# A graph network on one core: a sort's one-hot tables compared in f32, and registers of the message loop loaded one tile earlier

## The reference

```python
out = relu(n_feat @ lin0_w.T + lin0_b)
h = out
eh = relu(e_feat @ en1_w.T + en1_b)
w_e = (eh @ en2_w.T + en2_b).reshape(-1, D, D)
for _ in range(STEPS):                       # STEPS = 6
    msg = einsum('ei,eio->eo', out[src], w_e)
    agg = segment_sum(msg, dst, num_segments=n_nodes) + conv_bias
    m = relu(agg)
    h = gru_cell(m, h, gru_wih, gru_whh, gru_bih, gru_bhh)
    out = h
```

## Time and profile before

| | us |
|---|---|
| median of 3 runs | 36292.2 |
| lowest, highest | 36284.42, 36300.33 |
| the profiled execution | 36308.66 |
| its span, first to last instruction | 36306.9 |
| PE busy (matmuls) | 27537.1 |
| DVE busy | 25689.6 |
| ACT busy | 12361.2 |
| POOL busy | 28544.6 |

### The profile page before, as it was taken

The page is one execution under the profiler, slowest core; times in us unless marked ns, Lnnn a source line. Parts: engine busy times, 40 slices in busy tenths (PEclk is TensorE's granted clock), DMA queues, the critical chain, the costliest instruction groups (busy, mean ns, idle before and its releaser), DMA issues. The chain is left out here.

```text
span 36306.9 us, 436242 instructions
## 1 busy us (share of the span) xinstructions
PE 27537.1 (76%) x89048; PEld 15722.1 (43%) x89049; DVE 25689.6 (71%) x33878; ACT 12361.2 (34%) x38546; POOL 28544.6 (79%) x30158
## 2 busy tenths in 40 slices
PE   4443356655663333699999999999999999999999
PEld 2110034455663333444444444444444444454444
DVE  6654422222531211599999999999999999999998
ACT  0000011111200000255555555555555555555554
POOL 5777777677237677699979997999799979988997
PEclk6555566655655555799999999999999999999999
DMA  2221122211310010111111111111111111111111
GB/s 50 49 47 28 28 65 81 64 27 28 92 28 14 13 15 14 33 48 49 49 45 49 48 49 46 48 49 49 45 49 49 47 47 49 48 43 50 49 49 43
DMA packets 1456734, 1613.34 MB, mean 44 GB/s; under 512 B 955316, under 2 KB 1117095, under 8 KB 1348519
## 3 DMA queue, kind: packets, MB, share of 16 engines
q1 hardware_dynamic: 743256, 1078.25, 9.4%
q0 software_dynamic: 645120, 473.02, 7.5%
q10 hardware_dynamic: 68192, 60.43, 0.6%
HBM read 1365.34 MB, written 246.33 MB: 44 GB/s over the span
## 5 line engine op out<-in xcount | busy, mean ns | idle before, releaser
L2123 PE MATMUL l3m_p_w<-en,l3m_hid 128*128 128x512 f32 x39936 | 19533.7, 617 | 177.2 <-DVE l3m_prod L2204 101.8
L2193 DVE TENSOR_REDUCE l3m_xg<-l3m_prod 128x32 f32<-128x1056 f32 x9984 | 12427.1, 1245 | 0.3
L2014 POOL DMA_INDIRECT l3m_xg<-wide_table,l3m_mt x9984 | 9806.3, 982 | 2444.4 <-issue 1547.1
L2204 DVE TENSOR_TENSOR l3m_prod<-l3m_p_w,l3m_xg 128x704 f32<-128x704 f32 x9984 | 8830.7, 885 | 540.0 <-ACT l3m_rest L2067 531.3
L2023 POOL TENSOR_TENSOR l3m_prod<-l3m_rest,l3m_xg 128x320 f32<-128x320 f32 x9984 | 8752.3, 877 | 339.9 <-ACT l3m_rest L2067 159.8
L2123 PEld LDWEIGHTS l3m_p_w<-en,l3m_hid 128*128 128x128 f32 x39936 | 6784.6, 189 | 5141.2 <-issue 4794.7
L2067 ACT COPY l3m_rest<-l3m_p_w 128x320 f32<-128x320 f32 x9984 | 4256.4, 426 | 9432.2 <-PE l3m_p_w L2123 8296.3
L2139 PEld LDWEIGHTS l3m_p_sum<-room,l3m_apart 128*125 128x125 f32 x21120 | 3936.3, 197 | 5585.5 <-issue 5585.5
L2053 ACT ACTIVATE l3m_apart<-iota_lo,l3m_lo 128x125 f32<-128x125 f32 x9984 | 4000.3, 401 | 0.0
L2139 PE MATMUL l3m_p_sum<-room,l3m_apart 128*125 x21120 | 3318.9, 246 | 644.0 <-issue 619.2
L950 POOL DMA_INDIRECT l2a_rows<-table,l2a_mt x1664 | 1579.3, 949 | 1621.5 <-DMA l2a_mt<-dst_meta 1114.4
(11 more groups left out here) (392 smaller groups left out, 19630.3 us busy)
## 6 DMA issues: line engine op xcount, KB each, us to landing
l3m_hid<-hid_t SPq DMA_DIRECT2D x624, 1024.0 KB
l3m_xg<-wide_table,l3m_mt POOLq DMA_INDIRECT x9984
hid_t<-l_hid SPq DMA_DIRECT2D x110, 1024.0 KB, 4.0
order_src_bk<-dst_bucket SPq DMA_DIRECT2D x52, 1024.0 KB, 7.2
order_dst_bk<-src_bucket SPq DMA_DIRECT2D x52, 1024.0 KB
l_rec<-by_dst SPq DMA_DIRECT2D x110, 272.0 KB
l_xg<-table,l_mt POOLq DMA_INDIRECT x1760
l1a_xg<-table,l1a_mt POOLq DMA_INDIRECT x1760, 2.3
```

Of the source, the lines that this page charges most:

```text
L2014: pool.indirect_dma_start(xg[s][:, j, 0:2 * D], None, wide_table[:, :], bass.IndirectOffsetOnAxis(ap=mt[s][:, j, 0:1].bitcast(I32), axis=0 ...
L2123: ins = pe.matmul(p_w[j % 2][:, c * 512:(c + 1) * 512], hid[s][:, j * P:(j + 1) * P], en2[:, c * 512:(c + 1) * 512], start=True, stop=True)
L2193: dve.tensor_reduce(xg[s][:, j, 2 * D:3 * D], prod[j % RING][:, :, :], AX, ALU.add).then_inc(msgs, 1)
L2204: dve.tensor_tensor(prod[j % RING][:, 0:OWN, 0:D], o_i(p_w[j % 2][:, 0:OWN * D]), state_of(s, j, OWN), ALU.mult).then_inc(used, 1)
```

## The change

It does three things.

1. The bf16 ramp `iota_b16` is dropped, with the copy that filled it. The compares of `hit_lo` and `hit_b` read the f32 ramp `iota_lo`. Their second operands and their outputs stay bf16.
2. In the message loop the load of the 16 slot registers is taken out of `sum_up` into `slots_of`. In the groups it is called after tile `LATER - 1` = 7, behind the matmuls and the `sum_up` of that tile, and ahead of the matmuls of tile 8, at whose `sum_up` the registers are first used. The load of the row registers stays at the first `sum_up`.
3. For the last group, whose sums stand behind the loop, it is called ahead of them; in the tail it stays in `sum_up`.

```diff
@@ constants
-        iota_b16 = sb("iota_b16", [P, P], BF16)
...
-                    dve.tensor_copy(iota_b16[:, :], ramp[:, :])
@@ order, DVE
-                                        dve.tensor_tensor(hit_lo[h][:, :, :], iota_b16[:, None, 0:LO].broadcast_to(wide),
+                                        dve.tensor_tensor(hit_lo[h][:, :, :], iota_lo[:, None, :].broadcast_to(wide),
                                                           dst_lo16[:, cols][:, :, None].broadcast_to(wide), ALU.is_equal)
                                         wide = [P, HG, NB]
-                                        dve.tensor_tensor(hit_b[h][:, :, :], iota_b16[:, None, 0:NB].broadcast_to(wide),
+                                        dve.tensor_tensor(hit_b[h][:, :, :], iota_lo[:, None, 0:NB].broadcast_to(wide),
                                                           dst_b16[:, cols][:, :, None].broadcast_to(wide),
                                                           ALU.is_equal).then_inc(hits, 1)
@@ l3m, PE
+                        def slots_of(g):
+                            pe.load(slot_regs, slot_d[0:1, bass.ds(g * G, G)])
+
                         def sum_up(i, s, j, tail=False):
                             g = i * 2 + s
                             if j == 0:
-                                pe.load(slot_regs, slot_d[0:1, bass.ds(g * G, G)])
+                                if tail:
+                                    slots_of(g)
                                 pe.load(row_regs, window_d[0:1, bass.ds(g * G, G)])
...
                                 elif older:
                                     sum_up(i - 1, s, G - LATER + j)
+                                if newer and j == LATER - 1:
+
+                                    slots_of(i * 2 + (s - 1))
...
                         for j in range(G - LATER, G):
                             sum_up(TG // 2 - 1, 0, j)
+                        slots_of(TG - 1)
                         for j in range(G):
                             sum_up(TG // 2 - 1, 1, j)
```

## The result

The changed kernel takes 36113.58 us in the median of five runs (36105.1 to 36118.67) against 36292.2 for the kernel before (five runs, 36284.42 to 36300.33): 178.6 us less, a ratio of 0.995 with a 95% interval of 0.9939 to 0.9961. 36130 was forecast. The profiled execution took 36105.16 us.

The account below looks back on a forecast made before the run. PE's 1.2 us stop was taken to bound most of the message loop, POOL only 0.26 us a group behind; 6 x (22.6 + 4.5) = 163 us off, tables 0, gave 36130 us, forecast's own range 36110 to 36200, widened to 36070 to 36250.

Parts of the forecast that it names:

- The slots' load is hidden behind tile 7: Message loop: the load starts 0.3 us after tile 7's first matmul and ends near 20003.6, before tile 8 at 20003.94.
- the stop: PE's idle behind tile 8's matmuls from two register loads, costing 1.2 us a group; forecast to go to 0.
- PE starts a pass ahead and loses its lead: Message loop: PE some 4 us ahead, loses 3.9 us in 15 groups, then bounds the other 88 at 32.825 us.
- POOL then bounds every group at 32.57: Message loop after the change: POOL's 32.57 us a group is the largest, DVE at 31.9 and PE below that.
- One sign that was named: Message loop, profile after: ACT and DVE would wait for POOL instead of POOL waiting for ACT.
- 88 groups x 0.255 = 22.6 us a pass: Message loop: 88 groups a pass go from 32.825 to 32.57 us each, worth 22.6 us a pass.
- The 30 us that were put down as a lower bound: Message loop: should POOL's longer gaps ahead of gathers stay, 0.06 us a group, the gain is 30 us less.
- The end of a pass, 4.5 us: Last eight tiles of a pass, without gathers: PE and DVE's larger lead gains 4.5 us a pass, bounds 1 to 5.
- The lead's cap: Message loop with POOL as the bound: the most PE and DVE can run ahead of POOL, 4.6 us.
- The tables in f32, 0: First sort: f32 compares take the same time and still block POOL's scatters, 0 us; rival that f32 frees POOL, 0.05.
- The f32 addition that blocked a gather: Row of an f32 addition with both inputs in SBUF: the gather beside it takes 1.36 us, ending 0.82 us behind.
- the row of the two sorts: POOL's scatter means, 1.094 us in the first sort against 0.981 in the second: 188 us on the path.

Follow-up runs that it names:

- the second load behind tile 8: Changed kernel with the rows' load behind tile 8 issued for two register sets, slots' load staying behind tile 7: 36277.98 us, ratio 0.9988.
- the second profile of before: The kernel before, profiled once more with no edit: 36281.38 us, span 36279.6, gathers of 979 ns.
- the first set: One of three sets of runs, each on another chip beside the kernel before; here the slots' load alone took 36101.07 us, ratio 0.9951.
- the third: Set of runs on another chip, with the changed kernel once more at 36175.06 us against 36320.65 of before, ratio 0.996.
- the second set: Set of runs on another chip, with one output column moved from POOL to DVE in the changed kernel: 36061.83 us against 36296.6 of before.

## Why the prediction was right

- **The slots' load is hidden behind tile 7.** It was put at 0.3 us behind tile 7's first matmul and starts 0.28 behind; the stop went to 0 (idle of "issue" ahead of the sum-ups: 619 us in the profile before, none after). The runs with the tables alone and with the slots' load alone put all of the gain here, and the second load behind tile 8 brings the stop back.
- **PE starts a pass ahead and loses its lead.** The prediction inferred this from two paces. The trace of before has it: in the first pass ACT's copy ends 4.0 us ahead of POOL's product in the third group (15066.01 and 15070.04), and 0.36 us ahead in the seventeenth (15525.70 and 15526.05).
- **POOL then bounds every group at 32.57.** It does, at 32.54 to 32.59 by the length of the gathers. Moving a column to and from POOL, and the same edit on the kernel before, show it. One sign that was named did not show: the profile puts down ACT's waits to PE and DVE's to ACT, none of note to POOL. After the change DVE's instructions fill all of the 1000 us from 17000 to 18000 (975 in the second profile of before) and POOL's 913, so busy time alone would have pointed at DVE; the moved columns tell that it is POOL.
- **88 groups x 0.255 = 22.6 us a pass.** Between the two profiles with gathers of 979 ns it is 2888.6 - 2863.2 = 25.4 us a pass, 152 us in all. Between the two with 982 it is 2888.6 - 2868.3 = 20.3, and these are the gathers of the rows that the term came from: POOL alone needs 32.59 a group there, not 32.57. The 30 us that were put down as a lower bound, for POOL's long gaps, did not come: the gaps went with the waits for ACT.
- **The end of a pass, 4.5 us.** The lead's cap was worked out as 4.6 us and is 4.25. From the first product of the last group to the first of the next pass, the second profile of before and then the one after:

```profile
L2023 POOL TENSOR_TENSOR l3m_prod<-l3m_rest,l3m_xg x17: 861/869/887, 18356.9 to 18525.9; 128x320 f32<-128x320 f32 x17
```

```profile
L2021 POOL TENSOR_TENSOR l3m_prod<-l3m_rest,l3m_xg x17: 867/876/890, 18334.9 to 18499.9; 128x320 f32<-128x320 f32 x17
```

That is 169.1 and 165.0 us here, and 169.1 and 164.6 in the mean of the five such places: 4.5 us a pass, as forecast (4.2 with the long gathers). The loop as a whole is 179.7 us shorter; the spans are 176.2 apart because the loop starts 3.7 us later in the profile after.
- **The tables in f32, 0.** Shown by the run with them alone. The f32 addition that blocked a gather was the right row: had the change put the ramp in PSUM it would have been worth 195 us, where the row of the two sorts had said 188. On this the Trainium skill, SBUF — State Buffer, section "Who interferes with whom", says that a DVE instruction with two SBUF inputs contends with a GpSimd instruction that reads SBUF. The trace agrees for these scatters, whose indices lie in SBUF (3 us against 0.96); the same section's inference, that a tensor_tensor leaves descriptor generation alone, does not carry over to them.
- **The sum.** 163 us were forecast. 178.6 were measured for the change, 176.9 for the slots' load alone in the first set, and 145.6 for the change in the third. What the forecast did not have is that the gain itself hangs on the gathers' length. The 163 were worked out from a profile with gathers of 982 ns, and with these the loop became 145 us shorter (21139.5 to 20994.6 us, from POOL's first product to its last); with 979 it became 180 us shorter (21137.6 to 20957.9). That the forecast of 36130 came within 17 us of the median is in part luck: its term for the 88 groups was 14 us too large for its own gathers, and the profiled execution of the change had the short ones.

Open is what sets the gathers' length in an execution, and why POOL's gaps of up to 0.6 us come only where it keeps waiting for ACT.

## What to carry to other kernels

An engine's idle time is worth what the next bound leaves of it: 1.2 us of stop a group gave 0.23 to 0.29 with POOL close behind, 0.8 with POOL relieved of a column, and 0.65 us of the same kind gave nothing where another engine set the pace. Where a loop starts with one engine ahead, compare its pace in the first groups with that of the later ones: the first shows what the loop will run at when the later bound is taken away. And before an operand's type is changed for the sake of a neighbour engine, look for a row in which the new type already stands beside that neighbour.

## What the runs showed that was not expected

- POOL's indirect DMAs change their length by some 3 ns from one execution to another, all of an execution together: the 9984 gathers of the message loop take 9779 us in five of the profiles (979 ns each), 9785 to 9793 in the four of the second set (980 to 981) and 9805 to 9812 in the other five (982 to 983), and the scatters of the first sort 1091 to 1094 (the mean with the blocked ones). A kernel that POOL bounds feels it: the changed kernel's profiled executions have spans of 36103.4 and 36173.1, of which 37 us lie in the message loop and 33 ahead of it. The kernel before, bound by PE in most groups, moved by 2 us in the loop and 25 ahead of it (spans 36279.6 and 36306.9).
- With one input of DVE's compare in PSUM, POOL's scatters take 0.96 us beside it and the compare takes 2.24 as before: 195 us for one copy of 125 columns.
- A load of 16 registers into PE's sequencer takes 1.10 to 1.11 us, and one hides behind a tile of 1.95 us; two in a row do not. Two behind tile 7 stop PE for 0.65 us, two behind tile 8 for 0.9.
